# State-space mixer and gated MLP on one core: in the first block SyncE issues the second step's decay tables ahead of the residual rows

## What is computed

```python
x = L0_attn_hidden_states                      # (2, 1024, 512)
x = x + _L0_attn_ref(_layernorm(x, axis=-1), ...)
x = x + _L0_ffn_ref(_layernorm(x, axis=-1), ...)
...
# in the mixer
proj = hidden_states @ W_in * mup_vector
z, xBC, dt = jnp.split(proj, [D_SSM, D_SSM + CONV_DIM], axis=-1)
...
dt = jax.nn.softplus(dt + dt_bias).reshape(B, L, G, Hg)
dA = jnp.exp(dt * (-jnp.exp(A_log)).reshape(G, Hg))
...
state = state * dA_t[..., None, None] + (dt_t[..., None] * x_t)[..., None] * B_t[:, :, None, None, :]
y_t = jnp.einsum('bghps,bgs->bghp', state, C_t)
```

## Time and profile before

| | |
|---|---|
| median of 3 runs | 828.86 us (828.42 to 829.15) |
| the profiled execution | 825.1 us, of it the span 823.0 us |
| mean granted TensorE clock | 0.965 |
| PE busy | 748.8 us (91%) |
| DVE, ACT, POOL busy | 62%, 61%, 36% |

### The profile page before, as it was taken

The page is one execution under the profiler, slowest core; times in us unless marked ns, Lnnn a source line. Parts: engine busy times, 40 slices in busy tenths (PEclk is TensorE's granted clock), DMA queues, the critical chain, the costliest instruction groups (busy, mean ns, idle before and its releaser), DMA issues. The chain is left out here.

```text
span 823.0 us, 20282 instructions
## 1 busy us (share of the span) xinstructions
PE 748.8 (91%) x8464; PEld 615.0 (75%) x8464; DVE 512.5 (62%) x839; ACT 505.9 (61%) x963; POOL 298.0 (36%) x245
## 2 busy tenths in 40 slices
PE   5874999999999999999999997548989999999997
PEld 4864778788788788878888884436767887887886
DVE  6883976976976976976976966654622632542331
ACT  6984978978978978888888887024511321331330
POOL 2233366375275276276186175021001001002002
PEclk9986999999999999999999999868999999999999
DMA  9705054443443524423523425921003002102102
GB/s 298 214 2 154 12 117 117 78 112 107 94 98 104 126 66 113 129 68 104 136 66 96 117 66 159 401 59 47 26 16 124 17 5 93 56 0 74 28 1 77
DMA packets 39195, 77.67 MB, mean 94 GB/s; under 512 B 9408, under 2 KB 15040, under 8 KB 39104
## 3 DMA queue, kind: packets, MB, share of 16 engines
q1 hardware_dynamic: 38784, 75.84, 33.4%
q10 hardware_dynamic: 320, 0.52, 0.3%
HBM read 67.43 MB, written 8.92 MB: 93 GB/s over the span
## 5 line engine op out<-in xcount | busy, mean ns | idle before, releaser
L409 POOL TENSOR_TENSOR ring<-tokd,ring 128x1024 f32<-128x1024 f32 x64 | 121.9, 1918 | 198.0 <-ACT tokd L574 127.5
L1064 PE MATMUL ps_proj<-xn_hi,win_hi 128*128 128x256 f32 x608 | 179.2, 295 | 13.9 <-ACT dt_v L506 11.3
L1065 PE MATMUL ps_proj<-xn_lo,win_hi 128*128 128x256 f32 x608 | 172.8, 284 | 0.0
L1066 PE MATMUL ps_proj<-xn_hi,win_lo 128*128 128x256 f32 x608 | 172.4, 284 | 0.0
L1064 PEld LDWEIGHTS ps_proj<-xn_hi,win_hi 128*128 128x128 f32 x608 | 116.7, 192 | 28.2 <-issue 12.9
L1065 PEld LDWEIGHTS ps_proj<-xn_lo,win_hi 128*128 128x128 f32 x608 | 116.9, 192 | 0.3
L1066 PEld LDWEIGHTS ps_proj<-xn_hi,win_lo 128*128 128x128 f32 x608 | 116.8, 192 | 0.0
L799 DVE SCALAR_TENSOR_TENSOR cx<-cin,consts,cx 128x256 f32<-128x256 f32 x240 | 96.3, 477 | 0.0
L1367 POOL TENSOR_TENSOR res<-res,hidden 128x512 f32<-128x512 f32 x16 | 20.5, 1282 | 188.4 <-DVE hidden L1442 188.4
L1399 ACT ACTIVATE silu_g<-pb,scales 128x512 f32<-128x512 f32 x44 | 30.3, 688 | 94.4 <-PE pb L1511 94.3
L1511 PE MATMUL pb<-x1n_hi,wg_hi 128*128 128x512 f32 x176 | 70.4, 400 | 13.0 <-issue 13.0
(11 more groups left out here) (148 smaller groups left out, 1502.9 us busy)
## 6 DMA issues: line engine op xcount, KB each, us to landing
ring<-cum_dram SPq DMA_DIRECT2D x128, 256.0 KB, 4.9
xin<-x SPq DMA_DIRECT2D x8, 512.0 KB, 3.9
res<-x SPq DMA_DIRECT2D x32, 128.0 KB, 2.6
x_in_sb<-x_dram SPq DMA_DIRECT2D x4, 1024.0 KB, 5.8
res<-x_dram SPq DMA_DIRECT2D x16, 256.0 KB, 2.7
out<-res SPq DMA_DIRECT2D x16, 256.0 KB, 2.0
x_dram<-res SPq DMA_DIRECT2D x28, 128.0 KB, 2.4
wg<-gate_w SPq DMA_DIRECT2D x4, 704.0 KB, 9.8
```

The costliest lines, as they stand in the source:

```text
L409: pool.tensor_tensor(ring[:, g, :, :], own, ring[:, g, :, :], ALU.subtract).then_inc(diffed, 1)
L1064: pe.matmul(out, win_hi[:, k, cols], xn_hi[:, k, :], start=(k == 0), stop=False)
L1065: pe.matmul(out, win_hi[:, k, cols], xn_lo[:, k, :], start=False, stop=False)
L1066: made = pe.matmul(out, win_lo[:, k, cols], xn_hi[:, k, :], start=False, stop=(k == KT - 1))
```

## The change

In the first block, `load_res(0, 0)` moves from ahead of the four `load_cums(0, 1, g)` to behind them. It then stands directly ahead of `load_res(0, 1)`. The later blocks keep their order: x1's store of half 0, its load, the tables, x1's store of half 1, its load.

```diff
             def body(i, first, last):
                 if not first:
                     store_x1(i - 1, 0)
-                load_res(i, 0, first)
+                    load_res(i, 0, first)
                 for g in range(GROUPS):
                     load_cums(i, 1, g)
-                if not first:
+                if first:
+                    load_res(i, 0, first)
+                else:
                     store_x1(i - 1, 1)
                 load_res(i, 1, first)
                 if i + 2 < BLOCKS:
```

## The result

The changed kernel took 815.93 us in the median of 4 runs (815.67 to 816.90), the kernel before 828.64 in the same session (4 runs, 825.87 to 829.15). The ratio is 0.9856, with an interval from 0.9832 to 0.9879: faster, by 12.7 us. The forecast was 819.1, in a range from 817.9 to 821.9. So the sign is right, and the time lies 2 us under the range. The profiled executions tell another size: 825.1 us before and 815.7 after, 9.4 us, where the sum had 9.8.

What follows compares the result with a forecast made beforehand. It took step 1's decay tables, queued on SyncE behind the residual load, to bound the kernel from 66 to 84 us. A 10.5 us ceiling less 0.7 for a VectorE/GpSimd collision gave 9.8, so 828.86 became 819.1, range 817.9 to 821.9.

Steps and rivals of the forecast that it cites:

- What set the end.: From 66 to 84 us, all engines idle for step 1's decay tables, queued on SyncE behind `load_res`, which waits for L746.
- SyncE's moves cost nothing: SyncE's queue: residual rows issued behind slot 3's tables hold nobody up; without cover the price would be 1.65 us.
- ScalarE's order is the ceiling, 10.5 us; slots 0 and 1 are the ones that count: Block 1's `dt` follows `make_skip` and the Relus of slots 0 and 1: 65.46 in place of 75.96, at most 10.5 us.
- What is late next: the collision, 0.7 us: GpSimd's differences from 54.1 take turns with VectorE's L746 first piece, making `make_skip` 0.7 us late: shift 9.8 us.
- that rival's 1.8: Rival, chance 0.12: `normalise` takes turns with GpSimd's differences too; `make_skip` 1.8 us late, shift 8.7 us, 820.2 us.
- The clock on the carry, a rival at 0.20, 1 to 1.7 us: TensorE's lower clock after a 2.3 us pause falls on the carry; gain 8.1 to 9.1 us, 819.8 to 820.8; chance 0.20.
- TensorE's own half clock behind the pause is no gain: TensorE's first projection after the pause: its half clock is no further gain, as the carry of 84.31 waits for `xpad`.
- The sum: Whole kernel: 9.8 us saved; profiled execution 825.1 to 815.3, median 828.86 to 819.1; chance 0.44 within half a microsecond.
- 828.86 - 9.8 = 819.1: Last step: the median, 3.8 us above the profiled execution, loses the same 9.8 us, as each run has the same wait.

Runs made afterwards that it cites:

- E7: Changed kernel with the first block's residual rows put between the tables of slots 0 and 1; 827.4 us, ratio 0.9994 to the kernel before.
- E4: Changed kernel, GpSimd's first two differences of step 1 held until piece 11's low part, the last two until piece 13's; 816.18 us.
- E2: The changed kernel run again with no edit, in the second session; 818.12 us, ratio 0.9898 to the kernel before.
- E6: Changed kernel with the first block's residual rows put between the tables of slots 1 and 2; 822.06 us, ratio 0.9935 to the kernel before.
- E3: Changed kernel with GpSimd's first difference of step 1 waiting until VectorE's normalise of block 1 is done; 818.90 us.
- E12: Kernel before, with 84 overwritten products in TensorE's 11 us pause and 24 behind projection 2; 827.48 us, ratio 1.0019.
- E8: Kernel before, with 84 overwritten products of 256 columns in TensorE's 11 us pause; 830.5 us, ratio 1.0032.
- E11: E4's kernel with 24 overwritten products of 256 columns behind block 1's projection 2; 821.48 us, ratio 0.9930 to the kernel before.
- E10: E4's kernel run again, with the same holds on GpSimd's differences; 817.49 us.

## Why the prediction was right, and where it failed

- *What set the end.* Right: the tables behind `load_res`. E7 puts it to the test: with slots 1 to 3 behind the residual rows again, the time is that of before (0.9994, 0.9978 to 1.0010).
- *SyncE's moves cost nothing.* Right. The residual rows came at 67.18 and nobody waited.
- *ScalarE's order is the ceiling, 10.5 us; slots 0 and 1 are the ones that count.* Right for the ceiling: `dt` at 66.47 is a microsecond short of 65.46, and in E4, without the collision, it is at 65.27. A second limit stands close behind it, which the forecast didn't have: in E2's trace `dt` waits 0.45 us for the end of TensorE's projection and starts at 66.96. That only slots 0 and 1 count was said of `dt` and is right for it; E6 shows that slots 2 and 3 have some 4 us of their own (3.7 between the medians of one session), which the forecast needn't pay, since they came in time (69.07 for a Relu at 74.25).
- *What is late next: the collision, 0.7 us.* Its size is right (`make_skip` starts at 62.17 to 62.44 in the four traces, 1.0 to 1.2 us behind the 61.21, 0.3 to 0.5 more than the forecast had), its place is in the main not. I put it on L746's first piece, and gave `normalise` a chance of 0.12 because it has one SBUF input. Three of the four traces show it on both halves of `normalise`, 2.1 and 2.2 us each in place of 0.54 in the first; E2's shows it on one half and on L746's first piece. The price came out lower than that rival's 1.8, as both pieces of L746 then found GpSimd waiting for slot 2. The rule of the Trainium skill (SBUF — State Buffer, "Who interferes with whom") counts `tensor_scalar` among what can take the shared pair, if its operands meet certain conditions, and says that the one that comes second blocks; here the trace agrees, with 4.26 us against 1.00.
- *The clock on the carry, a rival at 0.20, 1 to 1.7 us.* It came in one of four traces of the changed kernel, with 0.9 us at the first store and nothing by the MLP's x. (By the forecast's own terms its lower price was 1.7 - 0.76 = 0.9, so 820.0 us and not 819.8.) In both traces of E4's kernel the carry was slower too (2.81, 2.51), and in E3's (3.31).
- *TensorE's own half clock behind the pause is no gain.* Right, by E12: with both pauses filled, and the full clock behind them, the time is 0.2 to 3.0 us over before's.
- *The sum.* 9.8 us on the trace; measured 9.4 in the two profiled executions, 9.6 at the first store of x1 in the mean of the traces (8.4 to 10.4 by pair), 9.6 at the MLP's x, and 9.3 between the medians of 76 and 22 executions (8.6 without the first session). The mechanism and, to a microsecond, the size were right.
- *The step that failed* is the last: "828.86 - 9.8 = 819.1", with a range built of the terms of the gain alone. It took the 3.8 us between the profiled execution and the median for a constant, and carried no term for where the kernel's executions lie. Measured was 815.93, 2 us under the lower bound of 817.9. What the runs show in its place is a spread of 5 to 8 us for each kernel. The 828.86 was the median of three executions that all lay in the upper part of it, at which the 825.1 of the profiled one already hinted. Of all 76, the median is 827.0; three drawn from them at random have a median of 828.86 or more in some 4 of 100 cases. From 827.0 the sum gives 817.2, against 817.7 for the 22. The first four of the changed kernel lie low in their spread (815.7 to 816.9; only five of the 18 later ones are at 816.9 or lower). The two together made 12.7 us out of 9.3. Whether both are luck is not shown: four of each drawn at random from all executions differ by 12.7 us or more in only 5 of 1,000 cases, and no run tells what else was particular to the first session. I had the gap of 3.8 us between profile and median before me, and took it for a constant. In the later sessions 818.1, 818.4 and 817.6 were measured, two of three inside the range; that they are inside is in part luck as well, since the 819.1 was built on a level for before that was 2 us too high.

What stays open: why the first session showed 12.7 us, and what sets the spread of 5 to 8 us. The MLP's part varies by 3 us between the traces of the two kernels, and goes with the granted clock of one stretch of it; what makes that clock fall in one execution and not in the next, no run took apart.

## What to carry to other kernels

In a queue that works in order, one instruction's wait is everybody's. Ask of each entry what stands behind it that doesn't need the wait; the order of need in the reader's program (here ScalarE's two Relus ahead of `dt`) tells which entry has to pass. A stall that goes also moves work beside other work: list which instructions now run together on VectorE and GpSimd. If the profiled execution lies four microseconds beside the median of three, the range has to hold that, whatever the sum says. And two traces of one program can be a microsecond or two apart before they reach the change: measure a shift from a common point.

## What the runs showed of the hardware

- VectorE's `tensor_scalar` on 128x512 float32 from and to SBUF took 0.54 us alone and 2.1 to 2.2 us when it met GpSimd's `tensor_tensor` of 1.90; a `scalar_tensor_tensor` of 0.29 with two SBUF inputs took 3.68 us when a GpSimd instruction of 3.78 had begun 0.24 us before it (E6).
- A kernel with a filled pause of TensorE can be slower. In E8 (2.7 us by its ratio) the lower clock moved behind the next pause, onto a carry of 3.49 us in place of 1.94, which cost 1.1 us to the first store of x1; in E11 (4 us over E10) TensorE stood for 2.97 us some 145 us later, with no link that the profile names.
- TensorE stood for 3.1 to 4.7 us, waiting for nothing that the profile shows, in every one of the fourteen traces, where the MLP's weights come in (DMA share 1.03 in the changed kernel's first). Full DMA engines alone don't do it (E10, 214.5 to 220.5).
- In one stretch of 40 us in the MLP the mean granted clock was 1.00, 0.96 or 0.91 in the fourteen traces, and from the issue of the MLP's x to the end they took 313.1, 314.0 to 315.0, and 315.3 to 317.6 us.
- The same program took from 823.3 to 831.5 us in 76 executions.
